# Transposing the attention probabilities by DMA instead of on TensorE, with row traffic on a second queue

## What is computed

```python
x = x + tanh(g_xattn) * attention(layernorm(x), ctx, ctx, w_q, w_k, w_v)   # causal
x = x + tanh(g_ffn) * ffn(layernorm(x))
# attention: q = query @ w_q; k = key @ w_k; v = value @ w_v
#   softmax(causal(q @ k.T / sqrt(512))) @ v
# ffn: gelu(x @ ternary(W1).T + b1) @ ternary(W2).T + b2
#   ternary(w) = clip(round(w / mean(abs(w))), -1, 1)
```

## Time and profile before

| | |
|---|---|
| timed runs | 1742.77, 1746.44, 1746.86 us; median 1746.44 |
| the profiled execution | 1744.55 us, span 1742.7 us, mean granted clock of TensorE 0.985 |
| PE | busy 1661.5 us (95% of the span) |
| DVE | busy 914.8 us (52%) |
| ACT | busy 659.8 us (38%) |
| POOL | busy 307.8 us (18%) |
| DMA transposes | 256, all of 128x512 float16, issued by SP |

### The profile page before, as it was taken

The page is one execution under the profiler, slowest core; times in us unless marked ns, Lnnn a source line. Parts: engine busy times, 40 slices in busy tenths (PEclk is TensorE's granted clock), DMA queues, the critical chain, the costliest instruction groups (busy, mean ns, idle before and its releaser), DMA issues.

```text
span 1742.7 us, 25225 instructions
## 1 busy us (share of the span) xinstructions
PE 1661.5 (95%) x9024; PEld 854.1 (49%) x9024; DVE 914.8 (52%) x1639; ACT 659.8 (38%) x1032; POOL 307.8 (18%) x341
## 2 busy tenths in 40 slices
PE   3699999999999999888999999999999999999998
PEld 1455655565555565454444444444444444444444
DVE  3666666565666666777544443444444444444432
ACT  1223232333323235332344444444444444444443
POOL 1111111111111111112112221222112211222210
PEclk8799999999999999999999999999999999999999
DMA  5233324343434247463221222122221222112210
GB/s 193 62 79 100 76 68 128 55 121 70 107 73 110 66 121 196 118 170 121 67 60 32 66 66 60 30 66 63 63 66 24 66 66 64 45 47 66 67 37 24
DMA packets 183830, 138.69 MB, mean 80 GB/s; under 512 B 144592, under 2 KB 144592, under 8 KB 182608
## 3 DMA queue, kind: packets, MB, share of 16 engines
q1 hardware_dynamic: 183184, 137.42, 29.5%
q10 hardware_dynamic: 576, 0.27, 0.1%
HBM read 70.53 MB, written 33.55 MB: 60 GB/s over the span
## 4 chain that ended last, share of the span: by engine, by line
PE 68%; issue 13%; DVE 12%; ACT 2%; SPq 2%; DMA 1%; POOL 1%; DVEq 0%; POOLq 0%; ACTq 0%
PE t_ps L835 13%; PE pT_ps L940 12%; PE s_ps L940 12%; PE v_ps L835 11%; PE o_ps L900 6%; PE v_ps L913 5%; PE s_ps L863 4%; PE t_ps L882 4%; DVE v_s L798 2%; DVE cmax L574 2%; DVE w_s L746 1%; DVE pT L653 1%; DVE negmax L662 1%; PE pT_ps L848 1%; DVE xn L614 1%
## 5 line engine op out<-in xcount | busy, mean ns | idle before, releaser
L772 DVE SCALAR_TENSOR_TENSOR v_s<-g,sc,v_s 128x512 f16<-128x512 f32 x256 | 248.1, 969 | 467.1 <-ACT v_s L499 463.7
L940 PE MATMUL pT_ps<-w_s,v_s 128*128 128x512 f16 x1024 | 265.6, 379 | 0.8
L940 PE MATMUL s_ps<-w_s,v_s 128*128 128x512 f16 x1024 | 262.8, 379 | 0.0
L835 PE MATMUL v_ps<-ctx_s,w_s 128*128 128x512 f16 x1024 | 241.9, 379 | 0.9 <-DVE w_s L746 0.9
L835 PE MATMUL t_ps<-ctx_s,w_s 128*128 128x512 f16 x1024 | 241.9, 379 | 0.0
L900 PE MATMUL o_ps<-v_s,pT 128*128 128x512 f16 x864 | 202.2, 386 | 28.5 <-DVE pT L653 28.5
L882 PE MATMUL t_ps<-xnT,a_s 128*128 128x256 f16 x1536 | 182.3, 276 | 24.5 <-ACT a_s L482 20.1
L863 PE MATMUL s_ps<-ctx_s,tT 128*128 128x512 f16 (+3 forms) x1152 | 198.1, 326 | 0.5 <-DVE tT L682 0.4
L913 PE MATMUL v_ps<-wv_s,ctx_s 128*128 128x512 f16 x768 | 178.7, 383 | 10.2 <-DVE ctx_s L546 10.2
L499 ACT ACTIVATE v_s<-g,sc 128x512 f16<-128x512 f32 x256 | 184.7, 721 | 8.3
L882 PEld LDWEIGHTS t_ps<-xnT,a_s 128*128 128x128 f16 x1536 | 151.4, 99 | 49.7 <-issue 26.1
(11 more groups left out here) (94 smaller groups left out, 1375.5 us busy)
## 6 DMA issues: line engine op xcount, KB each, us to landing
x_ring<-in_x SPq DMA_DIRECT2D x64, 256.0 KB, 3.0
raw<-in_ctxT SPq DMA_DIRECT2D x8, 2048.0 KB, 7.8
out_y<-x_ring SPq DMA_DIRECT2D x64, 256.0 KB, 3.2
raw<-out_y SPq DMA_DIRECT2D x64, 256.0 KB, 3.3
out_y<-v_s SPq DMA_DIRECT2D x64, 256.0 KB, 2.1
w_in<-in_w1T SPq DMA_DIRECT2D x16, 512.0 KB, 4.4
w_in<-in_w2T SPq DMA_DIRECT2D x16, 512.0 KB, 4.7
xnT<-xn_s SPq DMA_TRANSPOSE x128, 3.3
```

The lines of the kernel that those rows point to most:

```text
L772: v.scalar_tensor_tensor(out=g_s[:, f % 4, LO], in0=g32[:, f % 2], scalar=col(C_SG), in1=g_s[:, f % 4, HI], op0=ALU.mult, op1=ALU.subtract ...
L835: last_mm = mm(h_ps[f % 2], w1_s[:, c, (f % FC) * P:(f % FC + 1) * P], yT[:, (f // FC) % 2, a, c, :], start=(a == HI and c == 0), stop=(a ...
L940: last_mm = mm(y_ps[i], g_s[:, f % 4, a, i * P:(i + 1) * P], w2_s[:, f, :], start=(f == 0 and a == HI), stop=(f == FC - 1 and a == LO))
```

## The change

The probabilities are no longer transposed on PE. `p_s` and `pT` become rings of two, and SP issues two DMA transposes for each row (HI and LO, 128 by w*128) in `turn_p`, after the row's `p_split`, between the row transposes and the weight loads of the slot. The copy on DVE, the PSUM tile and the identity go; the PSUM space stays, as `e_ps`, for the start.

A row is finished in place, in `x_ring`, and `x2_ring` goes. ACT issues the row traffic: at the head of a slot the load of tile t+6 (`load_row`), which waits until the row that lay in that buffer, t-2, is stored; at the end of a slot, behind the sums of weights, the store of row t-1 (`store_row`), which waits for `o_done`.

On PE, the value matmuls of a slot now stand ahead of the output matmuls.

```diff
+            def turn_p(it, s):
+                r, w = s % 2, s % TB + 1
+                sp.wait_ge(p_split, it * BODY + s + 1)
+                sp.sem_inc(p_turn_issued, 1)
+                sp.wait_ge(pv_mm, it * BODY + s - 1 + PV0)
+                sp.sem_inc(p_turn_issued, 1)
+                for a in (HI, LO):
+                    sp.dma_start_transpose(pT[:, r, a, 0:w], p_s[:, r, a, 0:w * P]).then_inc(p_turned[r], 16)
             def slot(it, s, last=False):
                 t = it * BODY + s
                 if not last or t + XT_LEAD < NT + GT:
                     turn_row(it, s, last)
+                if not last or t < NT:
+                    turn_p(it, s)
                 if last:
                     for m, (at, _, _) in enumerate(W_STEPS):
                         if at == t:
                             load_weights(m)
-                if not last or t + 7 < NT:
-                    sp.wait_ge(o_done, t)
-                    sp.dma_start(x_ring[:, (s + 7) % 8], x_tiles[t + 7]).then_inc(x_in[(s + 7) % 8], 16)
-                sp.wait_ge(o_done, t)
-                sp.dma_start(out_tiles[t - 1], x2_ring[:, (s - 1) % 4]).then_inc(x2_stored[(s - 1) % 4], 16)
...
+            def load_row(it, s):
+                act.wait_ge(x2_stored[(s + 6) % 8], it * (BODY // 8) * 16 + ((s - 2) // 8 + 2) * 16)
+                act.sem_inc(row_issued, 1)
+                act.dma_start(x_ring[:, (s + 6) % 8], x_tiles[it * BODY + s + 6]).then_inc(x_in[(s + 6) % 8], 16)
+            def store_row(it, s):
+                act.wait_ge(o_done, it * BODY + s)
+                act.sem_inc(row_issued, 1)
+                act.dma_start(out_tiles[it * BODY + s - 1], x_ring[:, (s - 1) % 8]).then_inc(x2_stored[(s - 1) % 8], 16)
...
             def slot(it, s, last=False):
                 t = it * BODY + s
+                if s > 0 and (not last or t + 6 < NT):
+                    load_row(it, s)
                 if s >= 0 and (not last or t < NT):
                     softmax(it, s)
...
                 for m, n in w_turn(t, "S") if last else ():
                     sum_weight(m, n)
+                if s > 0:
+                    store_row(it, s)
...
-                if s >= 1:
-                    w = ((s - 1) % TB + 1) * P
-                    dve.wait_ge(p_tr, t)
-                    v.tensor_copy(pT[:, :, 0:w], pT_ps[:, :, 0:w]).then_inc(pT_ready, 1)
...
-                    dve.wait_ge(pv_mm, t)
-                    dve.wait_ge(x2_stored[(s - 1) % 4], it * (BODY // 4) * 16 + ((s - 1) // 4 + 1) * 16)
-                    v.scalar_tensor_tensor(out=x2_ring[:, (s - 1) % 4], in0=o_ps[:, :], scalar=osc[:, q:q + 1],
+                    dve.wait_ge(pv_mm, t + PV0)
+                    v.scalar_tensor_tensor(out=x_ring[:, (s - 1) % 8], in0=o_ps[:, :], scalar=osc[:, q:q + 1],
```

More of the change, by code:

```diff
@@ L149, in gated_block @@
         p_exp, p_hi, p_split = sem("p_exp"), sem("p_hi"), sem("p_split")
-        p_tr, pT_ready = sem("p_tr"), sem("pT_ready")
+        p_turned = [sem(f"p_turned{i}") for i in range(2)]
+        p_turn_issued, row_issued = sem("p_turn_issued"), sem("row_issued")
         pv_mm, o_inv, o_scaled, o_done = sem("pv_mm"), sem("o_inv"), sem("o_scaled"), sem("o_done")
-        x2_stored = [sem(f"x2_stored{i}") for i in range(4)]
+        x2_stored = [sem(f"x2_stored{i}") for i in range(8)]
         w_loaded = [sem(f"w_loaded{i}") for i in range(WR)]
@@ L226, in _ @@
             sp.dma_start(raw[:, :], ctx_batches[0].rearrange("p c s -> p (c s)")).then_inc(ctx_in, 16)
-            for t in range(3, 8):
+            for t in range(3, 7):
                 load_x(t)
@@ L272, in slot @@
                             load_weights(m)
-                if not last or t + 7 < NT:
-                    sp.wait_ge(o_done, t)
-                    sp.dma_start(x_ring[:, (s + 7) % 8], x_tiles[t + 7]).then_inc(x_in[(s + 7) % 8], 16)
-                sp.wait_ge(o_done, t)
-                sp.dma_start(out_tiles[t - 1], x2_ring[:, (s - 1) % 4]).then_inc(x2_stored[(s - 1) % 4], 16)
                 if s % TB == 7 and (not last or t + 9 < NT):
                     load_ctx(it * 2 + s // TB + 2)
+            for i in range(8):
+                sp.sem_inc(x2_stored[i], 16)
             for i in range(4):
-                sp.sem_inc(x2_stored[i], 16)
                 sp.sem_inc(y_stored[i], 16)
+            for r in range(2):
+                sp.sem_inc(p_turned[r], 32)
+            sp.sem_inc(pv_mm, PV0)
             sp.sem_inc(y_done, GT)
@@ L300, in _ @@
                         load_x2(i, i)
-            for i in range(4):
-                sp.wait_ge(x2_stored[i], 16 * (NT // 4 + 1))
+            for i in range(8):
+                sp.wait_ge(x2_stored[i], 16 * (NT // 8 + 1))
             def group(it, gg, last=False):
@@ L586, in scale_product @@
             def scale_product():
-                for n, half in enumerate((s_ps[:, :], pT32)):
+                for n, half in enumerate((s_ps[:, :], e_ps[:, :])):
                     dve.wait_ge(a_mm, n + 1)
@@ L842, in slot @@
                 i = s % TB
-                if s >= 1:
-                    pe.wait_ge(p_split, t)
-                    for a in (HI, LO):
-                        for j in range((s - 1) % TB + 1):
-                            tr = nc.tensor.transpose(pT_ps[:, a, j * P:(j + 1) * P], p_s[:, a, j * P:(j + 1) * P],
-                                                     ident[:, :])
-                    tr.then_inc(p_tr, 1)
                 if s >= 0 and (not last or t < NT):
@@ L889, in slot @@
                     hidden(1, 1, 0)
-                if s >= 1:
-                    pe.wait_ge(pT_ready, t)
-                    pe.wait_ge(v_split, t + 1 if not last or t < NT else NT)
-                    if last and t == NT:
-                        pe.wait_ge(o_done, NT - 1)
-                    jn, par = (s - 1) % TB, ((s - 1) // TB) % 2
-                    for n, (pa, va) in enumerate(PASSES):
-                        for j in range(jn + 1):
-                            last_mm = mm(o_ps[:, :], pT[:, pa, j * P:(j + 1) * P], v_s[:, par, va, j],
-                                         start=(n == 0 and j == 0), stop=(n == 2 and j == jn))
-                    last_mm.then_inc(pv_mm, 1)
                 if s >= -1 and (not last or t + 1 < NT):
@@ L915, in slot @@
                     last_mm.then_inc(v_mm, 1)
+                if s >= 1:
+                    pe.wait_ge(p_turned[(s - 1) % 2], p_turned_by(it, s - 1))
+                    pe.wait_ge(v_split, t + 1 if not last or t < NT else NT)
+                    if last and t == NT:
+                        pe.wait_ge(o_done, NT - 1)
+                    jn, par = (s - 1) % TB, ((s - 1) // TB) % 2
+                    for n, (pa, va) in enumerate(PASSES):
+                        for j in range(jn + 1):
+                            last_mm = mm(o_ps[:, :], pT[:, (s - 1) % 2, pa, j], v_s[:, par, va, j],
+                                         start=(n == 0 and j == 0), stop=(n == 2 and j == jn))
+                    last_mm.then_inc(pv_mm, 1)
             for s in range(FIRST_SLOT, 1):
```

32 lines of the change are left out of this document (15 added, 17 removed).

## The result

The changed kernel takes 1793.34 us (median of four runs, 1791.51 to 1796.23), the kernel before 1745.11 (four runs on the same chip): ratio 1.0279, 95% interval 1.0257 to 1.0300. It is slower by about 48 us; the forecast was 1784 within 1760 to 1825. The profiled execution took 1796.23 us (span 1794.4).

A forecast was written before the change was run, and what follows sets the result against it. TensorE was taken to bound slots 1 to 48, and a loop through SP's late weight loads slots 49 to 63. 1744.55 - 27 + 66 = 1783.6, said as 1784; eight in ten from 1760 to 1825.

The forecast's parts named there:

- the loop: Slots 49 to 63: exp, split, transposes, weight load, ternary step or sum, next exp; 258.4 us for 192.7, loss 66.
- The term of the transposes' issue: In the loop of slots 49 to 63: SP's issue of p's two transposes, proportional to width, 0.635 us a block.
- the estimate was 1757: Time with SP's transposes priced at 261 GB/s, 0.25 us a block pair, the last 15 slots 27 us shorter.
- the store behind the sums: Slots 49 to 52, on ScalarE: row store behind the sums, 3.2 us to land, row load, exp; 3.75 us a slot.
- The gain in the steady part: Slots 1 to 48: transposes leave TensorE and the copy's wait goes; 27 us gain, 15 to 34.
- ScalarE's new waits: Slots 1 to 48: row load waits for a store's landing ahead of exp; taken as 0, at most 11 us.
- The reduction: GpSimd, once a batch: 1.6 us gained from the copy's wait, 1.0 charged for the T split then late.
- the 24 us of the transposes: Slots 1 to 48: transposes leaving TensorE, 0.056 us each, 4.0 us a batch over 6 batches.
- FFN untouched: The FFN part, the last 900 us from 843.15 on, is not touched by the change.
- B: Rival, slots 49 to 63: weight loads run a slot ahead and are hidden, all eight batches gain; 1710 us, chance 0.08.
- C: Rival, slower still: p transposes at twice the price, 1844 us, or the clock staying at 0.50, 1858; chance 0.12.
- D: Rival: TensorE's transposes are worth the longer time, about 275 ns each; 1658 us, chance 0.02.

The follow-up runs named there:

- e1: The changed kernel with SP issuing a slot's weight loads ahead of the transposes of p in slots 49 to 63; 1731.79 us.
- e11: The changed kernel with 7 or 8 blocks transposed in every one of the last slots, the extra ones not read; last slots 247.0 us against 248.5.
- e10: e6 with the row load moved behind the slot's exp, copy of p and copy of T on ScalarE; 1721.32 us.
- e3: One part of the change alone: rows finished in place and moved by ScalarE's queue, p transposed on TensorE, matmuls in the old order; 1749.77 us.
- e4: The changed kernel with row loads and stores issued by SP, load at the slot's head, store at its end; 1777.43 us.
- e5: e1 with row loads and stores on SP's queue, load at the slot's head, store at its end; last slots 198.2 us against e1's 186.7.
- e9: e5 with the row load moved from the head of SP's slot to behind the weight loads; 1721.56 us.
- e12: The kernel before with the loop's reduction over partitions replaced by a copy of two columns; steady part 565.2 us against 575.0.
- e8: e1 with the loop's reduction over partitions replaced by a copy of two columns; steady part 549.1 us against 559.7.
- e2: The kernel before with SP waiting for the slot's split of p before its weight loads in slots 49 to 63; last slots 216.2 us against 192.7.
- e6: e1 with the last attention row's store moved behind the first two GELUs on ScalarE; 1726.62 us.
- e7: e1 with the row load on ScalarE behind the slot's exp and copy of p; 1730.80 us.

## Why the prediction was right, and which terms were off

**Slower, by the loop.** Right: the mechanism and its place are what the trace and e1 show, in all slots but one. Slot 53 is luck: 19.6 us for 18.5, but behind the reduction of the weight sums and not behind its chunk. The exps of slots 49 to 63 start at 644.09, 659.01, 673.14, 689.44, 703.06, 722.65, 741.97, 759.11, 772.94, 787.71, 804.11, 822.25, 839.66, 857.68 and 875.57. Slots 49 to 52: 59.0 us (forecast 62.8). Slots 53 to 62: 172.5 us (175.9), single ones 19.6, 19.3, 17.1, 13.8, 14.8, 16.4, 18.1, 17.4, 18.0, 17.9 for 18.5, 20.9, 20.0, 13.2, 12.8, 15.8, 17.0, 18.1, 19.2, 20.4. Slot 63: 12.5 for 15.2. The sum is 248.5 for 258.4, the lower edge of what was to show it. DVE's waits for chunks in slots 54 to 63 are 5.4 to 6.7 us, as the signs had it, but for slot 59 (2.1), where DVE had stood 3.7 us for POOL before, behind the second such reduction.

**The term of the transposes' issue was mis-sized.** I took it as proportional, 0.635 us a block: 45 us in 15 slots. It is nearly constant; the fifteen rows of line 277 sum to 38.6 us (2.40 to 2.62 us each, one 3.30), and e11 shows it: net, 6.5 of the 10 us by which the last slots came out short. From slot 54 on most misses have its shape: too little at small widths, too much at large ones. The end that I had named and left, 1.27 us each, was the right one. The Trainium skill's 261 GB/s (DMA: Bandwidth & Descriptors, "Latency and other measured facts"), by which the estimate was 1757, is a rate for what a transpose moves and does not describe these either: their issue hardly grows with the bytes.

**In slots 49 to 52 the store behind the sums was sized too large.** There the transposes took 10.0 us, 1.1 more than forecast, and yet the slots came out 3.8 us short. From the end of the last sum to the next exp I had 3.75 us a slot, 15 in all; it took 1.6, 1.6, 3.3 and 2.0, together 8.5. The store was issued while that sum still ran (in slot 51 at 685.12, the sum from 685.04), and the row load behind it followed 2.1, 2.2, 3.9 and 2.5 us later, where I had taken a landing of 3.2.

**The gain in the steady part: 27 forecast (15 to 34), 9.5 measured in the profile, 12.5 by the mean of the four kernels with the same code there.** Here the prediction was wrong beyond its own range, and its signs did not come: sixteen slots take 187 to 189 us, not 180 to 183, and TensorE is busy 95%, not 98%. Two steps failed.
- "ScalarE's new waits ... I take 0". They cost 8 us (562.5 against 554.5), likely most of it by the row load's place (e10), inside the bound of 11 that I had worked out from the landing of 5.5 us, and e3 has 5.9 for the same edit alone. I took the median landing, 3.2 us; in the slot where it matters it was 4.5. Not all of the 8 is explained by it: TensorE's waits on DVE's tT and v_s in the steady part are 14 to 18 us with the rows on ScalarE (e1, changed kernel) and 10 to 11 on SP (e4, e5, e9); TensorE's busy time there is 537 to 539 us in the same kernels, against 535 to 538.
- The reduction. I credited 1.6 us a batch for the wait that goes and charged 1.0 for what is late next. It costs 1.6 in the old order (e12) and 1.8 or more in the new (e8), so nothing was to be gained: 3.6 us of the 27.

What is left, 20.5 us (575.0 - 554.5), is the 24 us of the transposes less 3.5. Part of that is known: in the steady part TensorE idles 6.0 us in the loop's two turns, 3.6 before, and runs at a lower clock behind them (granted 0.83 over the 10 us behind each, 1.00 before). Why it idles longer, no run here tells; it is in e3 (5.6 us), with the transposes still on TensorE, and in e4, e5 and e9 (5.3 to 5.8), with the rows on SP, so neither edit alone is its cause. The kernels that have it (5.3 to 6.0 us) all finish rows in place, with eight landing semaphores for four; those without (before, e2, e12: 3.6 to 4.1) do not. That part wasn't run by itself, nor was the new place of the value matmuls. The clock behind the turns is not the same in all kernels with the longer idle: it is low (0.70 to 0.85) twice in the changed kernel, e3, e6, e10 and e11, once in e1, e4, e7, e8 and e9, and never in e5. Ten us at 0.83 cost an estimated 1.7 us, so this is part of the 6 us by which single profiles of one code differ.

**"FFN untouched" was wrong, +6.7 us.** I followed the moved store through the slots and not past the last one, where GELU's table load and the first two GELUs stand behind it. e6 gave 5.3 us back of the 7.6 that e1 has. The rest goes with the idle TensorE ahead of the seam. In e6 it waited 4.57 us for the last ternary step, where before it waited 0.92, and the granted clock over the FFN's first 12 us is 0.79 instead of 1.00: an estimate of 2.5 us from these two figures, for 2.3 measured (901.9 and 899.6). In the changed kernel the wait is 9.98 us and that clock 0.84.

**Rivals.** B (loads hidden) would have needed SP's other order; e1 is that kernel and got 1731.79 where B said 1710: its gain was the same overestimate, 27 for 15, and the FFN's 7.6. C: the granted clock over the last slots did fall, to 0.88, but those slots' length is set by the loop, and TensorE's 179 us of work fit into 248. D: TensorE's busy time in the steady part fell by 19.5 us, from 558.35 to 538.87, for 432 transposes, 0.045 us each, at a granted clock of 0.99 for 1.00; in e5, at 1.00, it is 534.55, which makes 0.055 us each. That is the 0.056 of the earlier trace rows and far from 0.275. The Trainium skill's figure of about 275 ns (TensorE: Matmul & The Clock Gate, "Part 4: PE-mode transpose") is not what they cost in this stream.

The forecast is only 9 us off because errors offset. Against the profiled executions: 16 us of gain too much (27 for 9.5 and the 1.4 of the start), 10 us of loss too much, 7 us forgotten; 16 - 10 + 7 = 13, and the median lies 3 us under the profiled execution.

## What to carry to other kernels

On a queue that issues in order, a DMA put ahead of others makes all of them wait for what it waits for: write the order down, and for each DMA behind it ask whether its consumer is in the same step; if so a loop closes, and one swapped pair of lines decided here between 2.8% slower and 0.8% faster. Follow a moved instruction to the end of the program and over its seams, not only through the loop. And look where a wait goes before you credit its end: here the reduction's was moved and not removed, and cost no less in the new place.

## What the runs showed of the hardware that was not expected

- A DMA transpose took SP 1.24 us at the median, and hardly less with one block of 128x128 than with eight (a pair 2.40 and 2.6 us); the landing's median moved from 2.7 to 3.0 us with 42 more blocks in 15 slots (e11). The price is not free of other traffic: eleven of the changed kernel's 64 pairs took 2.9 to 3.8 us, five of them 4 us behind the issue of a context load.
- In the changed kernel's last slots V's twelve matmuls took 5.28 us instead of 2.75 behind idles of 5.39, 6.92 and 5.01 us, 4.79, 4.38 and 4.11 behind 5.65, 6.13 and 3.33, and 2.75 behind 0.97, 2.14 and 3.06. At 5.28 they ran at the lower of the two clock levels (granted clock 0.50), at 2.75 at the higher; in between they changed on the way (0.57 to 0.66). While a loop over other engines is the bound that costs little; at the FFN's start, where TensorE is the bound again, it does.
- A row's store lands in 2.4 us at the median of the changed kernel, but in 4.5 in the slot of width 2, behind the context's 2 MB load (issued 9 us earlier) and beside two row transposes that took SP 3.48 us for the usual 2.5. Which of the two slows it wasn't tried.
